# A four-layer graph network on one core: the scores of a gathered chunk are kept after each gather instead of after every eighth

## The reference

```python
def _attention_aggregate(h_proj, sender, receiver, attn_vec, num_nodes):
    h_sender = h_proj[sender]
    h_receiver = h_proj[receiver]
    e = einsum('ehd,hd->eh', h_sender, attn_vec[:, :HD]) + einsum('ehd,hd->eh', h_receiver, attn_vec[:, HD:])
    e = leaky_relu(e, 0.2)
    e_max = segment_max(e, receiver, num_segments=num_nodes)
    alpha = exp(e - e_max[receiver])
    alpha_sum = segment_sum(alpha, receiver, num_segments=num_nodes)
    alpha = alpha / (alpha_sum[receiver] + 1e-08)
    return segment_sum(h_sender * alpha[..., None], receiver, num_segments=num_nodes)
h_in = _attention_aggregate(h_proj, src, dst, a_in, n)
h_out = _attention_aggregate(h_proj, dst, src, a_out, n)
combined = h @ W_self + h_in + h_out + bias        # then a layer norm with gamma and beta
```

## Time and profile before

| what | value |
|---|---|
| median of the runs | 4346.67 us |
| the profiled execution, its own time | 4351.3 us |
| its span, first to last instruction | 4349.5 us |
| TensorE busy | 2402.7 us (55%) |
| VectorE busy | 2404.7 us (55%) |
| GpSimd busy | 1621.1 us (37%) |
| ScalarE busy | 837.7 us (19%) |
| mean granted TensorE clock | 0.782 of full speed |
| gathers of line 1296 | 864, 816.4 us busy |
| reduces of line 1137 | 864, 532.4 us busy |

### The profile page before, as it was taken

The page is one execution under the profiler, slowest core; times in us unless marked ns, Lnnn a source line. Parts: engine busy times, 40 slices in busy tenths (PEclk is TensorE's granted clock), DMA queues, the critical chain, the costliest instruction groups (busy, mean ns, idle before and its releaser), DMA issues.

```text
span 4349.5 us, 54947 instructions
## 1 busy us (share of the span) xinstructions
PE 2402.7 (55%) x16100; PEld 1506.8 (35%) x16104; DVE 2404.7 (55%) x3420; ACT 837.7 (19%) x1390; POOL 1621.1 (37%) x1455
## 2 busy tenths in 40 slices
PE   1688777694989859410000000000796767996763
PEld 1234555442455434400000000000453665553663
DVE  8998888735120467500000000000799878999877
ACT  0494333201110120000000000000111542111542
POOL 6201333218777760066677677766100000000000
PEclk9899999997999979655555555555897599997597
DMA  1000111142534107143333433334300151000153
GB/s 55 0 0 27 45 45 41 63 154 59 161 73 96 24 8 160 28 106 97 103 104 105 98 104 99 105 103 97 28 0 0 51 177 47 0 0 0 37 175 99
DMA packets 195116, 301.54 MB, mean 69 GB/s; under 512 B 120540, under 2 KB 133818, under 8 KB 194922
## 3 DMA queue, kind: packets, MB, share of 16 engines
q1 hardware_dynamic: 138986, 175.88, 12.8%
q0 software_dynamic: 40512, 62.87, 8.2%
q10 hardware_dynamic: 15552, 61.94, 4.7%
HBM read 191.65 MB, written 88.01 MB: 64 GB/s over the span
## 4 chain that ended last, share of the span: by engine, by line
PE 40%; another core or an unknown queue 21%; DVE 19%; issue 14%; ACT 4%; DVEq 1%; DMA 0%; ACTq 0%; SPq 0%; PEldq 0%
PE PS L532 11%; PE PS L692 7%; PE PS L1101 6%; PE PS L879 5%; PE PS L1105 4%; ACT arena L508 3%; DVE arena L553 3%; PE PS L968 2%; DVE arena L1194 2%; DVE arena L1137 2%; PE PS L955 1%; PE PS L470 1%; DVE arena L368 1%; PE PS L1240 1%
## 5 line engine op out<-in xcount | busy, mean ns | idle before, releaser
L1137 DVE TENSOR_REDUCE arena<-PS 128x512 f32 (+1 forms) x864 | 532.4, 679 | 1156.0 <-remote 898.8
L1101 PE MATMUL PS<-big_id,arena 128*128 128x512 bf16 x864 | 356.9, 413 | 1137.3 <-issue 571.7
L1296 POOL DMA_INDIRECT arena<-T_att,idx x864 | 816.4, 945 | 395.2 <-issue 263.4
L532 PE MATMUL PS<-arena 128*128 128x400 f16 (+2 forms) x4320 | 772.8, 329 | 269.1 <-issue 114.0
L532 PEld LDWEIGHTS PS<-arena 128*128 128x128 f16 (+2 forms) x4320 | 520.8, 155 | 512.3 <-issue 349.3
L1472 POOL DMA_INDIRECT order<-arena x400 | 511.2, 1278 | 252.4 <-issue 252.4
L1101 PEld LDWEIGHTS PS<-big_id,arena 128*128 128x128 bf16 x864 | 83.8, 97 | 1280.4 <-DVE arena L1137 692.3
L553 DVE TENSOR_SCALAR arena<-arena 128x1600 f16<-128x1600 f16 x448 | 385.6, 904 | 64.5 <-PE PS L532 60.4
L1069 ACT COPY arena<-PS 12x1024 bf16<-12x1024 bf16 x108 | 108.1, 1001 | 1606.4 <-remote 926.2
L692 PE MATMUL PS<-arena 128*128 128x512 f16 (+1 forms) x1575 | 316.6, 361 | 95.5 <-issue 82.2
L1105 PE MATMUL PS<-arena,pick 128*128 128x128 bf16 x3456 | 356.7, 229 | 0.0
(11 more groups left out here) (254 smaller groups left out, 2876.7 us busy)
## 6 DMA issues: line engine op xcount, KB each, us to landing
spill<-arena SPq DMA_DIRECT2D x108, 560.0 KB
arena<-spill ACTq DMA_DIRECT2D x108, 560.0 KB, 3.6
arena<-A SPq DMA_DIRECT2D x50, 800.0 KB
A<-arena SPq DMA_DIRECT2D x50, 400.0 KB, 2.4
arena<-A SPq DMA_DIRECT2D x50, 400.0 KB
arena<-T_att,idx POOLq DMA_INDIRECT x864
order<-arena POOLq DMA_INDIRECT x400
T_att<-h SPq DMA_DIRECT2D x2, 1600.0 KB, 12.4
```

The costliest lines, as they stand in the source:

```text
L532: return t.matmul(where, lhsT, rhs, start=False, stop=True, skip_group_check=True)
L1101: t.matmul(PS[:, bank:bank + BANK], OHb[:, s, :], big_id[:, :].unsqueeze(1).to_broadcast([P, HEADS, P]), start=True, stop=False, skip_grou ...
L1137: v.tensor_reduce(cmax[d][:, :, bass.ds(i * SLOTS + half * GROUP + j, 1)].rearrange("p h k -> p (h k)"), PS[:, bank:bank + BANK].rearrange ...
L1296: p.indirect_dma_start(out=ring1[:, b, j, :], out_offset=None, in_=T_att[d][:, :], in_offset=bass.IndirectOffsetOnAxis(ap=idx[:, d, k:k + ...
```

## The change

`KEEPS` becomes `GROUP`, 8. Each cast now covers one chunk, 12 columns, and the order on GpSimd is: one gather of group n, the cast of one chunk of group n-1, the wait for its count, the next gather. The wait for the landing of group n-1 stands behind the first gather of group n. ScalarE's wait for a group's scores (line 1061) and the ring's wait (line 1293) count eight for each group. Nothing else differs.

```diff
@@ -1052,7 +1052,7 @@
-        KEEPS = 1
+        KEEPS = GROUP
 
         def top_act(a, d):
```

## The result

| | before | after |
|---|---|---|
| median of the runs | 4346.67 us | 3979.62 us (3968.97 to 3985.35, 4 runs) |
| the profiled execution's span | 4349.5 us | 3973.1 us |
| granted TensorE clock, mean | 0.782 | 0.795 |

The ratio is 0.915, with an interval of 0.9139 to 0.9162. The change takes 367 us off. The forecast was 785 us off, at 3562 us. The sign held. The size is that of the first rival, relief in part, whose bounds were 3768 and 4227 us.

What follows compares the result with a forecast made beforehand. GpSimd's gather stream was taken to delay TensorE's counts, pushing the attention behind it. With counts freed, 2493, 2814 and 3149 plus 381.2 give 3530, with 35 us of stalls 3565, adjusted to 3562 us; range 3475 to 4480.

Steps and rivals of the forecast that it cites:

- the first rival: TensorE's counts in the stream: relief only in part, 1.4 to 2.9 us a count, 3768 to 4227, so 4000 us; chance 0.16.
- What bounds the kernel: Middle 1200 us: GpSimd's gather stream delays TensorE's counts, so nearly the whole attention follows the stream.
- The cast, the turn, the group: GpSimd's stream: a 12-column cast takes 0.21 us, a gather-to-gather turn 1.42 us, a group of eight 11.66 us.
- The stream's end: GpSimd's gathers: stream takes 1281 us, last scores at 3139 instead of 3078, by itself a loss of 61 us.
- The 35 us of stalls: Some 220 gathers beside the rest of the first direction: VectorE's work adds 0.16 us each, moving 3530 to 3565.
- Above about 1.4 us between two DMAs nothing piles up: Gather stream: a turn of 1.42 us exceeds the 1.40 at which gathers pile up, so TensorE's counts come at once.
- The counterexample: Scatters of line 1472: 1.49 us apart as a rule, 1.65 on average, with TensorE 79% busy beside them.
- The first direction's maximum: VectorE's 416 chunks at 0.74 us each keep up with the stream; the maximum ends at 2493.
- The rest of the first direction: Work after that direction's maximum, beside the gathers: takes its undisturbed 320.6 us, ending at 2814.
- The second direction's maximum and the tail: End of the attention: maximum takes 330.6 us from 2814, ends at 3149 (3184 with stalls); what follows takes 381.2 us.
- The second: Rival, slower: TensorE's counts stay 11 to 15 us apart and the longer stream costs in full, 4404 us; chance 0.20.
- The third: Rival: each cast's count comes late, a group 19.6 us, stream end near 3975; 4366 to some 5200; chance 0.04.

Runs made afterwards that it cites:

- 440 columns: Kernel before with a memset of 440 uint8 columns behind every gather, which nobody waits for; 3700.8 us.
- The table: Both kernels and edits of them (own-cast wait removed, or 16 to 512 memset columns behind every gather), ordered by mean gather pace, 1.392 to 1.924 us; times 3621.6 to 4346.7 us.
- the second trace: Changed kernel, unchanged, run again beside the kernel before in another session; 3996.2 us, ratio 0.9195.
- the pairs in the kernel before: Kernel before with TensorE's and VectorE's counts of the maximum given for two chunks at a time, no pause or wait added; 4365.4 us.
- the run without the wait: Changed kernel without GpSimd's wait for each cast's own count, all else the same; 4286.1 us.

## Why the prediction was wrong, by its own steps

- **What bounds the kernel**: right. The stream's issue held TensorE's counts, the attention followed behind it, and slowing the stream alone (440 columns) gave 646 us.
- **The cast, the turn, the group**: right. 0.21, 1.43 and 11.74 to 11.78 us against 0.21, 1.42 and 11.66. No cast of 12 columns was in the trace of before; the slope between 96 and 3200 columns carried it.
- **The stream's end**: 3192 instead of 3139. 8 to 12 us come from the group. The rest lies in the second direction's groups, 1.572 us per gather on average, beside the first direction's remaining work (groups 56 to 100). The 35 us of stalls that I set for this would put it at 3174.
- **"Above about 1.4 us between two DMAs nothing piles up"**: this step failed. It took the pace at which a saturated stream settles for a threshold above which the counts are free. My reading, not shown by itself, is that 1.40 is where nothing is left over and each count needs room of its own. At 1.473 there was 0.08 us per gather to spare, and the counts came late by less, not on time. The counterexample that I used, the scatters, was at 1.65 us on average and 1.49 at the least. The table frees the first maximum at 1.52 and leaves only the stream's end to decide from 1.55 on, between the two figures: the row that I leaned on bounded the threshold from above and said nothing of 1.42.
- **The first direction's maximum**: 2658 instead of 2493, 165 late. The group's pace explains some 6 of it, TensorE's counts the rest: 5.9 us at the median from a chunk's last product to its reduce, with four banks in turn, where I had put nothing.
- **The rest of the first direction**: 602 us instead of 320.6, the largest miss, 282 us (2735 and 548 us in the second trace, so that the two misses are 447 us together here and 469 there). I let it run at its undisturbed length beside the gathers, and priced only what it does to the stream, not what the stream does to it: from TensorE's product of line 1250 to VectorE's reduce of line 1203 it is 10.0 us at the median, against 0.17 undisturbed. Its waits from 2660 to 3260 in the changed kernel:

```profile
DVE arena L1203 <- remote: 176.3, 36, 6.5
PEld PS L1240 <- DVE arena L1194: 160.3, 34, 6.9
PE PS L1240 <- DVE arena L1194: 156.4, 33, 6.8
ACT arena L1272 <- remote: 112.1, 23, 7.7
```

- **The second direction's maximum and the tail**: 331 and 381 us, as put (330.6 and 381.2). But the maximum started at 3261 instead of 2814, after the stream, so nothing of it was hidden. Forecast end of that maximum 3184, measured 3592: 408 us late, and 3973.1 is 408 above the forecast span of 3565.
- **The rivals**: the first one held, in mechanism ("a little may always be queued"). It had 0.16. That its 4000 lies near 3980 is luck: it is the middle of two sums, 3768 and 4227. Its sum at 1.4 us a count comes near for the first maximum (2620, measured 2659), but it too lets the rest of the direction take its undisturbed 320 us. Its "ten counts make eight chunks" isn't how the hold works either, as the pairs in the kernel before show. The second, no relief because the margin is too thin, is nearly what the run without the wait shows at 1.414 us (4286). The third, each cast's count late by 1 us or more, didn't come: a group is 0.12 us above the sum in all.
- **The rule that I set the counts against**: the Trainium skill, page "SBUF — State Buffer", section "Who interferes with whom", says that TensorE and ScalarE never wait on anyone. The section is about SBUF's ports. Here TensorE's completions were seen late in six of the eight sessions and not in two; for ScalarE's no row shows it. The Trainium skill's page "VectorE: DVE Perf Modes", section on the TRN2 errata, warns that increments at a high rate from one engine can deadlock another, and asks to space them where several engines give many. Nothing here deadlocked, and eight times as many from GpSimd did no harm: its turn was 1.43 us, as costed.

The chances: 0.57 for a forecast that needed a margin of 1% to 4% to be enough was too much, the more so as a rival stated just that.

## What to carry to other kernels

When a queue's pace holds up others, the pace of the saturated stretch is the point of no surplus, and not the point of relief. Look for the least pace at which the trace shows the others free, and leave more than a few per cent. Then price both ways of a new overlap: what the work does to the stream, and what the stream does to each stage of the work that now lies beside it. And before an engine is slowed on purpose, compare the kernel in several sessions: here a pause of 0.40 us behind each gather gains 17% where the counts are held, and one of 0.37 us, with the counts in pairs, costs 4% where they aren't.

## What the runs showed of the hardware

- Beside indirect DMAs that GpSimd issues at a mean of 1.39 us, TensorE's semaphore counts come late, and VectorE's don't: VectorE's unnamed waits at the maximum are 14.6 us long on average, while TensorE starts 0.06 us after a reduce's end. At 1.47 they are 1.9 us, and from 1.55 on the stream's end alone sets the time. The count of DMAs matters, not their rows (64 or 128, both 4347 us), and the mean over a group more than each spacing (3817 us with gathers at 1.25 us and a pause of 1.8 us after eight).
- The same program on the same inputs ran at 4347 or at 3456 us, stable within a session, with the hold present or absent. The traces with the hold lack a quarter of the semaphore updates from 900 to 1850 us that the others have. Which of the two brings the other, if either does, isn't known.
- A gather of 64 rows costs GpSimd 0.908 us, one of 128 rows 0.944: nearly all of it is per instruction.
- A second cost of VectorE's work beside the gathers shows right after the first maximum: the small casts grow from 0.21 to 1.04 us and the gathers from 0.95 to 1.44 while VectorE runs its scans of lines 1163 and 1164 (2660.88 to 2668.3). The longest gather, 3.52 us, lies beside VectorE's two-input operations of lines 1175 and 1178, 3.1 us each.

```profile
2660.88 1.05 DVE L1163 TENSOR_TENSOR_SCAN arena<-arena 128x416 f32<-128x416 f32 x1
...
2663.61 1.04 POOL L1306 CAST W<-arena 128x12 bf16<-128x12 f32 x1
2664.92 1.44 POOL L1296 DMA_INDIRECT arena<-T_att,idx  x1 [0.27 <-POOL W L1306]
```
